# The final norm of a transformer layer with experts: statistics, roots and adds in another order

## The reference

```python
scores = jax.nn.softmax(xf @ gate_w.T, axis=-1)
vals, idx = jax.lax.top_k(scores.T, k)            # every expert takes its 512 best rows
y = layer norm of xf[flat_idx] with ln_w, ln_b
h = gelu(einsum('knd,nfd->knf', y, fc1s) + b1s)   # 256 -> 1024
out = (einsum('knf,ndf->knd', h, fc2s) + b2s) * kept_w[..., None]
xf = xf.at[flat_idx].add(out.reshape(k * n, d))
...
x = x + _layernorm(xf)                            # the final norm: eps 1e-5, no weights
```

## Time and profile before

| | us |
|---|---|
| median of 3 runs (808.90, 808.92, 810.62) | 808.92 |
| the profiled execution | 808.87 |
| its span | 807.1 |
| TensorE busy | 702.6 (87%) |
| VectorE busy | 616.0 (76%) |
| ScalarE busy | 470.4 (58%) |
| GpSimd busy | 365.2 (45%) |

### The profile page before, as it was taken

The page is one execution under the profiler, slowest core; times in us unless marked ns, Lnnn a source line. Parts: engine busy times, 40 slices in busy tenths (PEclk is TensorE's granted clock), DMA queues, the critical chain, the costliest instruction groups (busy, mean ns, idle before and its releaser), DMA issues. The chain is left out here.

```text
span 807.1 us, 15731 instructions
## 1 busy us (share of the span) xinstructions
PE 702.6 (87%) x5799; PEld 573.8 (71%) x5799; DVE 616.0 (76%) x1282; ACT 470.4 (58%) x749; POOL 365.2 (45%) x364
## 2 busy tenths in 40 slices
PE   7998999999999999999999979333599999999920
PEld 6867768778768778688687668333498889999820
DVE  4976678888798798798789687778667667767681
ACT  3655747867857857858758745362155544445560
POOL 4264306517517616616625514200444456544673
PEclk9999999999999999999999999655599999999975
DMA  8000010011011011101110112420236664555694
GB/s 250 28 2 2 1 53 2 28 53 54 28 53 53 26 52 53 52 27 52 52 53 3 53 54 73 133 65 0 87 100 149 152 160 110 112 141 158 183 224 96
DMA packets 50702, 61.00 MB, mean 76 GB/s; under 512 B 9312, under 2 KB 44896, under 8 KB 50656
## 3 DMA queue, kind: packets, MB, share of 16 engines
q1 hardware_dynamic: 42400, 46.45, 18.0%
q0 software_dynamic: 7296, 13.77, 9.0%
q10 hardware_dynamic: 960, 0.17, 0.1%
HBM read 39.28 MB, written 21.10 MB: 75 GB/s over the span
## 5 line engine op out<-in xcount | busy, mean ns | idle before, releaser
L2056 PE MATMUL pF<-w,h 128*128 128x256 f32 x448 | 106.1, 383 | 0.0
L1093 POOL DMA_INDIRECT kp<-row_scratch,idx_g x32 | 41.6, 1299 | 117.4 <-issue 60.3
L2056 PEld LDWEIGHTS pF<-w,h 128*128 128x128 f32 x448 | 82.0, 190 | 12.9 <-issue 3.4
L871 ACT ACTIVATE h<-pX,b1cur 128x512 f32<-128x512 f32 x64 | 44.2, 690 | 62.6 <-DVE b1cur L1836 45.4
L2455 PE MATMUL pX<-w_lo,h_hi 128*128 128x256 f32 x256 | 73.3, 286 | 0.8 <-issue 0.8
L960 POOL TENSOR_SCALAR ve<-mv 128x4 f32<-128x4 f32 x36 | 8.5, 235 | 143.9 <-DVE mv L1171 143.0
L2455 PE MATMUL pX<-w_hi,h_lo 128*128 128x256 f32 x256 | 72.6, 283 | 0.0
L2455 PE MATMUL pX<-w_hi,h_hi 128*128 128x256 f32 x256 | 72.5, 283 | 0.0
L1792 DVE TENSOR_TENSOR h_lo<-h,h_hi 128x512 fp32r<-128x512 f32 x64 | 42.9, 691 | 29.1 <-ACT h_hi L863 29.1
L1101 POOL DMA_INDIRECT acc_scratch<-qp,idx_s x28 | 53.2, 1900 | 22.4 <-DVE qp L1818 18.1
L1993 PE MATMUL pX<-x2T_hi,w_lo 128*128 128x512 f32 x128 | 51.5, 402 | 1.6 <-DVE x2T_lo L1862 1.6
(11 more groups left out here) (407 smaller groups left out, 2091.7 us busy)
## 6 DMA issues: line engine op xcount, KB each, us to landing
kp<-fc1T SPq DMA_DIRECT2D x8, 1024.0 KB, 7.6
w<-fc2T SPq DMA_DIRECT2D x8, 1024.0 KB, 8.7
xin<-video SPq DMA_DIRECT2D x8, 512.0 KB, 3.6
x<-video SPq DMA_DIRECT2D x7, 512.0 KB, 4.6
out<-x SPq DMA_DIRECT2D x7, 512.0 KB, 3.0
acc_scratch<-xf SPq DMA_DIRECT2D x7, 512.0 KB, 2.9
row_scratch<-y SPq DMA_DIRECT2D x7, 512.0 KB, 3.0
kp<-acc_scratch SPq DMA_DIRECT2D x4, 512.0 KB, 5.9
```

Source lines behind the costliest of these rows:

```text
L871: nc.scalar.activation(h[:, n, :], pM[n % M_SLOTS], ACT.Gelu_apprx_tanh, bias=b1cur[:, n:n + 1]).then_inc(he_ready, 1)
L1093: pool.indirect_dma_start(xg[:, g, :], None, row_d, bass.IndirectOffsetOnAxis(ap=idx_g[:, g:g + 1], axis=0)).then_inc(gathered, 16)
L2056: ins = nc.tensor.matmul(pF[m][:, half * D:(half + 1) * D], h[:, k, tok(2 * m + half)], w2[:, k, :], start=(k == 0), stop=(k == FC - 1))
```

## The change

VectorE adds epsilon itself, in `stats_last` and for the rows, so `root_last` is one power. On VectorE the statistics of all blocks 2 to 7 come ahead of the second half of the last expert's rows; shift 7 stands inside that half. GpSimd's order becomes: roots 0, 1, add 0, roots 2, 3, add 1, roots 4, 5, add of 2 and 3 in one DMA, roots 6, 7, add of 4 and 5 in one DMA, add 6, add 7, the rows' root. There are thus 6 add DMAs instead of 8, of the same bytes. The body of the two halves moves into functions unchanged.

```diff
-            sp.wait_ge(out_done, 16 * (B + GT))
+            sp.wait_ge(out_done, 16 * (B - 2 + GT))
...
             def root_last(j):
-                var, ve_, rs = (mv[0][:, :, 1], ve[0][:], rstd[0][:]) if j == "rows" else (mvl[:, j, :, 1], vel[:, j], rsl[:, j])
+                ve_, rs = (ve[0][:], rstd[0][:]) if j == "rows" else (vel[:, j], rsl[:, j])
                 pool.wait_ge(vl_ready, nth[j])
-                nc.gpsimd.tensor_scalar(ve_, var, LN_EPS, None, ALU.add).then_inc(vel_ready, 1)
-                pool.wait_ge(vel_ready, nth[j])
                 nc.gpsimd.tensor_tensor(rs, ve_, mhalf[:], ALU.pow).then_inc(rl_ready, 1)
 
-            def add_last(j):
-                pool.wait_ge(nl_ready, j + 1)
-                pool.dma_start(out_n[j], acc_s[j // LQ][:, j % LQ], accum_op=ALU.add).then_inc(out_done, 16)
+            def add_last(j, blocks=1):
+                pool.wait_ge(nl_ready, j + blocks)
+                pool.dma_start(out_n[j:j + blocks].rearrange("b p t d -> p b t d"), acc_s[j // LQ][:, j % LQ:j % LQ + blocks],
+                               accum_op=ALU.add).then_inc(out_done, 16)
 
             root_last(0)
             root_last(1)
             pool.wait_ge(fix_in, 16 * 2 * GT)
             add_last(0)
             root_last(2)
+            root_last(3)
             add_last(1)
-            for j in range(3, B):
-                root_last(j)
-                add_last(j - 1)
+            root_last(4)
+            root_last(5)
+            add_last(2, 2)
+            root_last(6)
+            root_last(7)
+            add_last(4, 2)
+            add_last(6)
+            add_last(7)
             root_last("rows")
-            add_last(B - 1)
             pool.wait_ge(fix_ready, 1)
-            pool.wait_ge(out_done, 16 * B)
+            pool.wait_ge(out_done, 16 * (B - 2))
...
             def stats_last(j):
...
-                ins.then_inc(vl_ready, 1)
+                done.link(ins)
+                nc.vector.tensor_scalar(vel[:, j], mvl[:, j, :, 1], LN_EPS, None, ALU.add).then_inc(vl_ready, 1)
...
+            def last_rows(e, m):
+                if m == 0:
+                    dve.wait_ge(b2e_in, 16 * (e + 1))
+                    dve.wait_ge(wcur_ready, e + 1)
+                biased_rows(e, m)
+                weighted_rows(e, m)
+                if m == 1:
+                    shift_last(B - 1)
+                dve.wait_ge(fix_in, 16 * 2 * GT)
+                dve.wait_ge(og_ready, e * GT + 2 * m + 2)
+                a = acc_g[:, 2 * m:2 * m + 2]
+                done.link(nc.vector.tensor_tensor(a, a, og[:, 2 * m:2 * m + 2], ALU.add))
...
                     stats_last(0)
                     stats_last(1)
                     shift_last(0)
+                    last_rows(e, 0)
+                    shift_last(1)
+                    stats_last(2)
+                    for j in range(3, B):
+                        stats_last(j)
+                        shift_last(j - 1)
+                    last_rows(e, 1)
+                    return
...
             experts(dve, expert)
-            for j in range(LQ, B):
-                stats_last(j)
-                shift_last(j - 1)
             for t in range(TT):
                 ins = nc.vector.bn_stats(st[0][:, t, :], acc_g[:, t, :])
             done.link(ins)
-            shift_last(B - 1)
             for t in range(TT):
                 ins = nc.vector.bn_aggr(mv[0][:, t, :], st[0][:, t, :])
-            ins.then_inc(vl_ready, 1)
+            done.link(ins)
+            nc.vector.tensor_scalar(ve[0][:], mv[0][:, :, 1], LN_EPS, None, ALU.add).then_inc(vl_ready, 1)
```

More of the change, by code:

```diff
@@ L348, in build @@
         w2_hi_ready, w2_ready, h_hi_ready, h_lo_ready = sem("w2_hi_ready"), sem("w2_ready"), sem("h_hi_ready"), sem("h_lo_ready")
-        stl_ready, vl_ready, vel_ready, rl_ready, nmr_ready, nl_ready = (
-            sem("stl_ready"), sem("vl_ready"), sem("vel_ready"), sem("rl_ready"), sem("nmr_ready"), sem("nl_ready"))
+        stl_ready, vl_ready, rl_ready, nmr_ready, nl_ready = (
+            sem("stl_ready"), sem("vl_ready"), sem("rl_ready"), sem("nmr_ready"), sem("nl_ready"))
         last_order = [0, 1, 2, 3, 4, 5, 6, 7, "rows"]
@@ L1783, in shift_last, with biased_rows, weighted_rows @@
                                                op1=ALU.mult).then_inc(nmr_ready, 1)
+            def biased_rows(e, m):
+                dve.wait_ge(m_ready, e * M_JOBS + J_MY + m + 1)
+                nc.vector.tensor_tensor(og[:, 2 * m:2 * m + 2, :], pM[2 + m].rearrange("p (a b) -> p a b", a=2),
+                                        b2cur[:].unsqueeze(1).to_broadcast([P, 2, D]), ALU.add).then_inc(yo_ready, 1)
+            def weighted_rows(e, m):
+                dve.wait_ge(yo_ready, e * 2 + m + 1)
+                for g in (2 * m, 2 * m + 1):
+                    nc.vector.tensor_scalar(og[:, g, :], og[:, g, :], wcur[:, g:g + 1], None, ALU.mult).then_inc(og_ready, 1)
+            def last_rows(e, m):
[10 more added lines that the diff above has]
+                done.link(nc.vector.tensor_tensor(a, a, og[:, 2 * m:2 * m + 2], ALU.add))
             def expert(e, after):
```

## The result

The changed kernel is **slower: 1.0029 times the kernel before, 95% interval 1.0021 to 1.0037** (20 runs of each). Its median is 813.0 us, that of before, run beside it, 810.32. The three runs shown ahead had given 808.92, so 1.4 us of the distance between 810.0 and 813.0 is the level of before and not the change. The profiled execution of the changed kernel took 814.35 us with a span of 812.6.

What follows compares the result with a forecast made beforehand. The last block's accumulating DMA landing bounds the end: stream 795.29 plus 0.3 for the pair's issue gives 795.6, 1.1 later than 794.47. So 808.87 + 1.1 = 810.0 us, range 806.7 to 812.0.

Steps and rivals of the forecast that it cites:

- the one on the queue of transfers: Last blocks' add DMAs: six blocks in one stream from the pair's issue at 777.94, landing at 795.29 before the pair's extra.
- the pair's own issue: Issue of a two-block add DMA on GpSimd: 0.3 us extra, between bounds of nothing and 0.93.
- the higher service of 2.64: Transfer time per block as mean of the last four landing intervals, instead of 2.45; would add 0.95 us.
- Rival B: First pair's issue: first byte waits for all 256 descriptors, a second 0.93 us; 810.6 or 811.6 us; chance 0.25.
- Epsilon on VectorE: Block statistics on VectorE: epsilon costs 0.21 us a block, 1.99 instead of 1.78; the first half isn't later.
- GpSimd's and ScalarE's schedules: Roots, adds and normalising of the last blocks: first pair leaves at 777.94, last add at 785.6, 3.3 us earlier.
- The loads, TensorE and the rows' norm: Work beside the block adds: loads land by 772.4, TensorE's later reading costs nothing, rows' norm covered by 5 us.
- Rival A: Stream of add transfers is bound by its issues, so it ends 3.3 us earlier: 805.6 us; chance 0.20.
- Rival C: Add transfers: latency is paid per transfer, two fewer save 5.2 us on the forecast: 804.8 us; chance 0.03.
- The level: Time of the kernel before, taken as 808.92 us, the median of three runs; the sum starts from the profile's 808.87.

Runs made afterwards that it cites:

- e1: The changed kernel with each pair issued as two single adds at the same place; 1.0035 of the kernel before.
- e3: The kernel before with only epsilon moved to VectorE, orders and single adds as before; 1.0009 of the kernel before.
- e9: The changed kernel with epsilon back on GpSimd, orders and pairs as in the change; 1.0019 of the kernel before.
- e2: The changed kernel with single adds, each as early as its block allows, VectorE's program unchanged; 1.0003 of the kernel before.
- e8: The changed kernel with single adds as early as their blocks allow and epsilon back on GpSimd; 0.9982 of the kernel before.
- r3: Repetition of e2, the changed kernel with early single adds and epsilon on VectorE; 0.9997 of the kernel before.
- r4: Repetition of e8, the changed kernel with early single adds and epsilon on GpSimd; 0.9988 of the kernel before.
- e6: e2 (changed kernel, early single adds) with add 1 directly behind add 0, ahead of root 2; 1.0013 of the kernel before.
- e12: e8 (early single adds, epsilon on GpSimd) with add 1 ahead of root 2; 1.0005 of the kernel before.
- e4: The changed kernel without block 4's add, block 5 alone leaving in the second pair's place, output incomplete; 0.9998 of the kernel before.
- e10: e2 with VectorE's last addition of the rows waiting until all block adds have landed; 1.0021 of the kernel before.
- e13: The changed kernel with adds 2 and 3 single behind roots 4 and 5, pair 4, 5 kept; 1.0007 of the kernel before.
- e7: The kernel before with only the pairs, epsilon on GpSimd and VectorE's order as before; 1.0037 of the kernel before.

## Why the prediction was wrong

The measured 813.0 lies outside the range of 806.7 to 812.0, and the move was larger than the forecast's 1.1 us: 0.0029 of 810 is 2.35 us. By the medians it is 2.7. The direction and the mechanism held, the sizes didn't.

| term, + us | predicted | first profile | second profile |
|---|---|---|---|
| the first pair leaves | 11.32 | 11.23 | 11.59 |
| its flight | 7.85 | 8.2 | 8.3 |
| the four blocks behind it | 9.8 | 10.2 | 10.4 |
| last landing | 28.97 | 29.65 | 30.25 |
| against before (27.85, 28.04) | +1.1 | +1.8 | +2.2 |

- **The failed step is the one on the queue of transfers**, "777.94 + 5.1 + 5 x 2.45", with the 0.3 of the pair's own issue. From the issue of the first pair to the last landing it gave 17.65 us; the two profiles have 18.42 and 18.66, so it was 0.8 to 1.0 us too small. The prediction's own check showed most of this: the same formula gave before a landing at 793.8, and 794.47 was measured. The sum then set the formula's 795.6 against the measured 794.47. Formula against formula is 795.6 - 793.8 = 1.8 us, what the first profiles show. I had put the higher service of 2.64 only into the range.
- Where the missing time lies: the engines' own step is 2.49, not 2.45 (the first engines to finish the single blocks behind the pairs stand 2.48 to 2.50 apart in both profiles of the change), which is 0.2 of it. The first pair flies 0.4 to 0.5 longer, and the engines stand empty ahead of it for 0.75 and 0.9 us, not 1.5, since block 1 keeps them busy for 3.4 to 3.6 us instead of 2.45. The four blocks behind the pair take 0.4 and 0.55 longer: a block lands when the slowest of 16 engines is done, and the spread grows over them from 0.60 to 0.83 and from 0.61 to 0.72; in the second profile even the first engine finishes the second pair 0.3 late. In a full queue an engine that was held up didn't catch up: in e1 the spread stays at 2.02 to 2.03 over the last four blocks. In the kernel before the last adds leave 2.3 to 2.7 us apart, 2.49 on average, and its arrivals lie within 0.2 to 0.6 us from block 1 on.
- The pair's own issue was of the right size: GpSimd needs 1.20 to 1.24 us instead of 0.84 to 0.91, and the first packet moves 1.8 us after the issue, for a single 1.5. Rival B's mechanism is there with a third of its price. Its 1.7 to 2.7 us above before hold the measured 2.35, but not for its reason.
- Epsilon on VectorE: the pace of 1.99 us is exact. That it costs nothing beyond it isn't confirmed. Every comparison has the same sign: 0.0009 (e3 to before), 0.0006 and 0.0010 (the change to e9), 0.0021 and 0.0009 (e2 to e8, r3 to r4), 0.0008 (e6 to e12). Only e8 against e2 is clear of zero by itself (0.0021, with about 0.0016 of uncertainty from the two intervals). Weighted by their intervals the comparisons have a mean of about 0.0011 with 0.0006 of uncertainty: by this estimate epsilon is 0.4 to 1.4 us of the change's 2.35. How it would arise isn't known. The issues don't show it, since e2's last add leaves 0.65 us before e8's; there the difference sits in the stall at +23.5 that e8 and r4 don't have. It remains open.
- GpSimd's and ScalarE's schedules held: the adds behind the first were forecast, on the scale, at 7.33, 11.32, 15.4, 17.3 and 19.0 and left at 7.25, 11.23, 15.23, 16.66 and 18.62. The loads, TensorE and the rows' norm were covered, as said; the rows' last addition ends at 793.6, 6.5 us ahead of the last landing.
- Rival A is refuted: the last add leaves 3.65 us earlier on the scale and lands 1.8 later, and e4's timed runs gain a block's service with no issue moved. Rival C is refuted by e1: two transfers fewer than its singles gave nothing (1.0029 against 1.0035, intervals that overlap), not 5.2 us. The Trainium skill's rule to batch to 1 MiB (DMA: Bandwidth & Descriptors, section Bandwidth) brings nothing here: with two singles of 512 KB in flight (issued 2.3 to 2.7 us apart, 5.6 to 5.8 us of flight) the engines already have a share of 1.07.
- The level: I took the median of three runs of before, 808.92, as its level; 20 runs gave 810.32, with runs from 808.82 to 812.54. The range would have held the time on the old level: 1.0029 x 808.92 = 811.3. It should have been wider by that. Some of this scatter arises ahead of everything that the change moves: over the 17 profiles VectorE's first step on the last rows lies anywhere from 766.62 to 770.52, and TensorE ends the wait for it each time.

Not settled: why single packets stall for about 2 us at the same place in all three profiles of e2's order of adds (e2, r3, e10). It was not tried to give the blocks another place in SBUF, or the adds another split over engines.

## What to carry to other kernels

Where transfers with a service time of their own close a kernel, the end is about the first issue behind the last hole plus the work queued behind it. An earlier last issue was worth nothing here (3.65 us earlier, landed 1.8 later). An earlier first one was worth 0.9 to 1.5 us of 1.9 in e13, and nothing where it pushed the later issues back (e6, e12). One transfer made to wait for its neighbour so that both could go together cost that wait. If a formula is used for the kernel after, set it against the same formula for the kernel before, and price the landing by the slowest of 16 engines. The two kernels whose last issues follow the service closely (before 2.49 us apart on average over the last four, e8 2.46 over the last five) had smaller spreads than e2 with 2.24; no run varied this alone, so it isn't shown to be the cause. Take the level of the kernel before from more than three runs when 0.2% matters.

## What the runs showed of the hardware

- A 512 KB accumulating DMA from SBUF to HBM takes each of the 16 engines 2.49 us (8 packets of 4 KB, a step of 0.31 us each, 0.33 by the packets' own records; 211 GB/s together). The loads of `acc_scratch` reach twice that: 406 to 416 GB/s from 766 to 770 us in the kernel before.
- After a hole the packets take longer: the median of the first 16 is 0.5 to 1.1 us instead of 0.33 (the change, its repetition, e1, e4, e7, e9).
- A 1 MB add occupies GpSimd for 1.20 to 1.24 us, a 512 KB one for 0.84 to 0.91: the second 512 KB cost 0.3. Its first packet moves 1.8 us after the issue instead of 1.5.
- Single packets took 1 to 2.5 us in most profiles, up to four at once; with a full queue the delay is carried to the end (spreads of 1.9 to 2.5 us in e1, e2, r3, e4, e6, e10 and e12).
